# Cross attention with routing: where the routing pieces, the slot writes and GpSimd's elementwise work stand in a period

## The reference, cut to what matters

```python
q = split(x @ Wq + bq); k = split(ctx @ Wk + bk); v = split(ctx @ Wv + bv)
probs = softmax(q @ k.T / 4)            # layer 0: masked scores
x = layernorm(x + (probs @ v) @ Wo + bo)
scores = sigmoid(x @ gate_w.T)          # layer 1; layer 0: softmax of the best two
idx = top_k(scores + bias, K)           # the experts of a row
pos = cumsum(onehot(idx)) - 1           # the row's place within its expert
xe[idx, pos] = x                        # the rows written out by slot
```

## Time and profile before

| | us |
|---|---|
| median of 3 runs (lowest, highest) | 3422.43 (3417.75, 3429.29) |
| the profiled execution | 3419.93 |
| its span, first to last instruction | 3418.2 |
| PE, DVE, ACT, POOL busy | 2593.2, 2067.1, 1100.1, 817.1 |
| mean granted clock of TensorE, share of full speed | 0.872 |

### The profile page before, as it was taken

The page is one execution under the profiler, slowest core; times in us unless marked ns, Lnnn a source line. Parts: engine busy times, 40 slices in busy tenths (PEclk is TensorE's granted clock), DMA queues, the critical chain, the costliest instruction groups (busy, mean ns, idle before and its releaser), DMA issues. The chain is left out here.

```text
span 3418.2 us, 51809 instructions
## 1 busy us (share of the span) xinstructions
PE 2593.2 (76%) x17697; PEld 2118.0 (62%) x17698; DVE 2067.1 (60%) x4570; ACT 1100.1 (32%) x1952; POOL 817.1 (24%) x932
## 2 busy tenths in 40 slices
PE   4788786799999599988888989776758878747500
PEld 3666664455555499988888989755635555536400
DVE  5888885345555476666666665465536676635554
ACT  2334342344444222211111112123625454425400
POOL 0000000111111152222121020252112444332575
PEclk8999997899999699999999999888869888758855
DMA  1100020534432300012011010210055544327887
GB/s 50 34 18 21 18 71 28 76 56 63 66 54 32 111 31 31 28 61 90 25 61 61 31 61 28 57 54 20 0 82 88 91 75 64 48 49 201 215 119 90
DMA packets 201924, 210.31 MB, mean 62 GB/s; under 512 B 39889, under 2 KB 188152, under 8 KB 201808
## 3 DMA queue, kind: packets, MB, share of 16 engines
q1 hardware_dynamic: 166352, 142.53, 20.2%
q0 software_dynamic: 18432, 36.94, 6.2%
q10 hardware_dynamic: 17024, 29.36, 2.5%
HBM read 103.42 MB, written 67.90 MB: 50 GB/s over the span
## 5 line engine op out<-in xcount | busy, mean ns | idle before, releaser
L1143 DVE TENSOR_REDUCE x_nmx<-x_ps 128x4 f32<-128x1024 f32 x256 | 313.1, 1223 | 376.0 <-PE x_ps L879 374.8
L1497 PE MATMUL m_gu<-m_x_hi,m_w_hi 128*128 128x256 f32 x1632 | 464.8, 285 | 28.0 <-DVE m_x_lo L1563 17.5
L1497 PE MATMUL m_gu<-m_x_hi,m_w_lo 128*128 128x256 f32 x1632 | 459.9, 282 | 0.0
L1497 PE MATMUL m_gu<-m_x_lo,m_w_hi 128*128 128x256 f32 x1632 | 459.5, 282 | 0.0
L1535 ACT ACTIVATE m_sg<-m_gu 128x256 f32<-128x256 f32 x408 | 156.7, 384 | 754.7 <-PE m_gu L1497 754.7
L1047 ACT ACTIVATE x_pt<-x_ps 128x1024 f32<-128x1024 f32 x256 | 262.1, 1024 | 298.4 <-PE x_ps L879 295.9
L1569 DVE TENSOR_TENSOR m_h<-m_sg,m_gu 128x256 f32<-128x256 f32 x408 | 171.5, 420 | 306.6 <-ACT m_sg L1535 304.4
L1497 PEld LDWEIGHTS m_gu<-m_x_hi,m_w_hi 128*128 128x128 f32 x1632 | 312.0, 191 | 32.7 <-DVE m_x_lo L1563 17.9
L1497 PEld LDWEIGHTS m_gu<-m_x_hi,m_w_lo 128*128 128x128 f32 x1632 | 311.9, 191 | 0.0
L1497 PEld LDWEIGHTS m_gu<-m_x_lo,m_w_hi 128*128 128x128 f32 x1632 | 311.5, 191 | 0.0
L1486 PE MATMUL m_yp<-m_w_hi,m_h_hi 128*128 128x256 f32 x816 | 244.4, 299 | 80.2 <-DVE m_h_lo L1571 80.2
(11 more groups left out here) (301 smaller groups left out, 5477.1 us busy)
## 6 DMA issues: line engine op xcount, KB each, us to landing
m_x<-xs SPq DMA_DIRECT2D x68, 256.0 KB, 2.8
ys<-m_y SPq DMA_DIRECT2D x67, 256.0 KB, 2.2
x_qpack<-x_qh SPq DMA_DIRECT2D x128, 128.0 KB, 4.0
x_kpack<-x_kh SPq DMA_DIRECT2D x128, 128.0 KB, 4.3
xs<-zero SPq DMA_DIRECT2D x8, 1024.0 KB, 5.1
x_cx<-in_ctx SPq DMA_DIRECT2D x32, 256.0 KB, 5.3
x_qpack<-x_ql SPq DMA_DIRECT2D x64, 128.0 KB, 5.1
x_kpack<-x_kl SPq DMA_DIRECT2D x64, 128.0 KB, 5.3
```

What stands on the lines that cost most here:

```text
L1143: dve.tensor_reduce(nmx[:, n % U, t, 0:HEADS].rearrange("p (m q b) -> p m q b", m=2, q=QUADS)[:, :, j, :], ps[:, QUERY:QUERY + 2].rearrang ...
L1497: ins = pe.matmul(gu[:, m % 4, n, :], wp[n][:, c, m * P:m * P + P], xp_[:, c, :], start=(c == 0 and k == 0), stop=(c == KC - 1 and k == 2))
```

## The change

It moves pieces and adds waits; no arithmetic is added or removed. DVE: `place` goes one period later, between maximum 0 and maximum 1; `choose` is cut at the one-hot rows, of which the second part (`one_hot`) stands ahead of maximum 5; `weigh_experts` moves ahead of maximum 6; `take_logits` reads the logits in both layers. PE: `turn_rows`, `route`, `output`, `rank`, `weigh(k, 1)` and `key_scores(l, 7)` change places; ACT follows. POOL: the eight slot writes of a batch come a period later in two lots of four, one behind `low_queries`, one behind `rstd_of`; and each of the three large operations first waits until the scores of a certain group are ready, which is when that group's maximum begins (group 2, 4 and 5). One period is added for the drain.

```diff
--- before.py
+++ after.py
@@ -709,7 +709,7 @@
         ctx_v = d["ctx"].rearrange("(k p) n -> p k n", p=P)
         shared_v = st.xsh.rearrange("(n p) c -> p n c", p=P)
 
-        PERIODS = range(-1, B + 3)
+        PERIODS = range(-1, B + 4)
 
         def blocks(n):
             return slice(TB * n, TB * n + TB)
@@ -785,43 +785,52 @@
 
         @block.gpsimd
         def _(pool):
+            def beside_maximum(q, g):
+
+                if 0 <= q < B:
+                    pool.wait_ge(s_ready, GROUPS * q + g + 1)
+
             def low_queries(n):
                 pool.wait_ge(qh_ready, n + 1)
                 if n:
                     pool.wait_ge(pack_loaded[(n - 1) % PACKS], 16 * PACK_DMAS * ((n - 1) // PACKS + 1))
+                beside_maximum(n - 1, 2)
                 pool.tensor_tensor(ql[:], qf[:], qh[:].bitcast(F32), ALU.subtract).then_inc(ql_ready, 1)
 
             def low_keys(n):
                 pool.wait_ge(kh_ready, n + 1)
+                beside_maximum(n - 1, 4)
                 pool.tensor_tensor(kl[:], kf[:], kh[:].bitcast(F32), ALU.subtract).then_inc(kl_ready, 1)
 
             def add_bias(n):
                 if n >= U:
                     pool.wait_ge(xn_ready, n - U + 1)
+                beside_maximum(n + 2, 5)
                 pool.tensor_tensor(y[:, n % U], st.res[:, blocks(n), :], rows[:, 1:2, :].to_broadcast([P, TB, D]),
                                    ALU.add).then_inc(xb_ready, 1)
 
             def rstd_of(n):
                 pool_rstd(pool, st, var, rstd, n % U, varr, rstdr, epsr, n + 1)
 
-            def slots_out(n):
+            def slots_out(n, t):
                 pool.wait_ge(dst_ready, n + 1)
                 pool.sem_inc(st.pool_passed, 1)
-                for t in range(TB):
-                    for j in range(topk):
-                        pool.indirect_dma_start(
-                            out=st.xs1, out_offset=bass.IndirectOffsetOnAxis(ap=st.slot1[:, TB * n + t, j:j + 1], axis=0),
-                            in_=st.res[:, TB * n + t, :], in_offset=None, bounds_check=DUMP1 - 1,
-                            oob_is_err=False).then_inc(sent, 16)
+                for j in range(topk):
+                    pool.indirect_dma_start(
+                        out=st.xs1, out_offset=bass.IndirectOffsetOnAxis(ap=st.slot1[:, TB * n + t, j:j + 1], axis=0),
+                        in_=st.res[:, TB * n + t, :], in_offset=None, bounds_check=DUMP1 - 1,
+                        oob_is_err=False).then_inc(sent, 16)
 
             pool.wait_ge(w_loaded, 16 * 4)
             for p in PERIODS:
                 at(p + 1, low_queries)
+                if not masked:
+                    at(p - 4, slots_out, 0)
                 at(p + 1, low_keys)
                 at(p - 2, add_bias)
                 at(p - 2, rstd_of)
                 if not masked:
-                    at(p - 3, slots_out)
+                    at(p - 4, slots_out, 1)
             if not masked:
                 pool.wait_ge(sent, 16 * TB * topk * B)
 
@@ -967,16 +976,16 @@
                 at(l, weigh, 2)
                 at(a, turn_in)
                 at(k, turn_maxima)
+                at(l, key_scores, 7)
+                at(q, query_scores, 0)
+
+                at(a, project_queries)
                 at(r, turn_rows)
-                at(q, query_scores, 0)
-
-                at(l, key_scores, 7)
-                at(a, project_queries)
                 at(q, query_scores, 1)
 
                 at(l, weigh, 3)
+                at(k, key_scores, 0)
                 at(r, route)
-                at(k, key_scores, 0)
                 at(q, query_scores, 2)
 
                 at(k, key_scores, 1)
@@ -994,12 +1003,12 @@
                 at(q, query_scores, 5)
 
                 at(k, key_scores, 4)
+                at(l, output)
+                at(r, rank)
+                at(q, query_scores, 6)
+
+                at(k, key_scores, 5)
                 at(k, weigh, 1)
-                at(l, output)
-                at(q, query_scores, 6)
-
-                at(k, key_scores, 5)
-                at(r, rank)
                 at(q, query_scores, 7)
             if masked:
                 pe.wait_ge(counted, 1)
@@ -1075,31 +1084,31 @@
                 at(l, keep_values, 2)
                 at(a, keep_rows)
                 at(k, keep_maxima)
+                at(l, weights, 7)
+
+                at(a, keep_queries)
                 at(r, keep_normal)
-
-                at(l, weights, 7)
-                at(a, keep_queries)
 
                 at(l, keep_values, 3)
                 at(k, weights, 0)
+
+                at(k, weights, 1)
                 if not masked:
                     at(r, gates)
-
-                at(k, weights, 1)
                 at(a, keep_keys)
 
                 at(k, weights, 2)
                 at(k, keep_values, 0)
+
+                at(k, weights, 3)
                 if masked:
                     at(r, gates)
-
-                at(k, weights, 3)
                 at(l, keep_scaled)
 
                 at(k, weights, 4)
+
+                at(k, weights, 5)
                 at(k, keep_values, 1)
-
-                at(k, weights, 5)
 
         @block.vector
         def _(dve):
@@ -1168,13 +1177,16 @@
             def spread(v, shape):
                 return v.unsqueeze(3).to_broadcast(shape)
 
+            def take_logits(n):
+                dve.wait_ge(lg_ready, n + 1)
+                logits = bank(ROUTE)[:, :, 0:experts]
+                if masked:
+                    dve.tensor_copy(lg[:, :, 0:experts], logits).then_inc(lg_taken, 1)
+                else:
+                    dve.tensor_scalar(sc[:], logits, -1.0, EXP_MAX, ALU.mult, ALU.min).then_inc(lg_taken, 1)
+
             def choose(n):
-                u, here = n % U, blocks(n)
-                logits = bank(ROUTE)[:, :, 0:experts]
-                chosen = st.expert0[:, here, :] if masked else ixf[:]
                 if masked:
-                    dve.wait_ge(lg_ready, n + 1)
-                    dve.tensor_copy(lg[:, :, 0:experts], logits).then_inc(lg_taken, 1)
                     dve.wait_ge(lg_taken, n + 1)
                 else:
                     dve.wait_ge(e_ready, n + 1)
@@ -1190,6 +1202,10 @@
                     s.mark(dve.max_index(ix8[:, t, :], mx8[:, t, :], lg[:, t, :]))
                 if masked:
                     dve.tensor_tensor(tmp[:, :, 0], mx8[:, :, 1], mx8[:, :, 0], ALU.subtract).then_inc(earg_ready, 1)
+
+            def one_hot(n):
+                u, here = n % U, blocks(n)
+                chosen = st.expert0[:, here, :] if masked else ixf[:]
                 s.after(s.n)
                 s.do(dve.tensor_copy(chosen, ix8[:, :, 0:topk]))
                 s.do(dve.tensor_tensor(oh[:], st.iota[:, 0:ecols].unsqueeze(1).unsqueeze(1).to_broadcast([P, TB, topk, ecols]),
@@ -1215,12 +1231,6 @@
                     s.do(dve.tensor_scalar(tmp[:, :, 0], tmp[:, :, 0], 1e-12, None, ALU.max))
                     s.do(dve.reciprocal(tmp[:, :, 1], tmp[:, :, 0]))
                     s.do(dve.tensor_tensor(gt[:], gt[:], tmp[:, :, 1:2].to_broadcast([P, TB, topk]), ALU.mult))
-
-            def exponents(n):
-                dve.wait_ge(lg_ready, n + 1)
-                if n:
-                    dve.wait_ge(hit_ready, n)
-                dve.tensor_scalar(sc[:], bank(ROUTE)[:, :, 0:experts], -1.0, EXP_MAX, ALU.mult, ALU.min).then_inc(lg_taken, 1)
 
             def place(n):
                 here = blocks(n)
@@ -1249,20 +1259,20 @@
                 a, q, l, r = p + 1, p, p - 2, p - 3
                 at(r, normalize)
                 at(q, maxima, 0)
+                at(r - 1, place)
                 at(q, maxima, 1)
-                if not masked:
-                    at(r, exponents)
+                at(r, take_logits)
                 at(q, maxima, 2)
                 at(r, choose)
                 at(q, maxima, 3)
                 at(l, scaled)
                 at(q, maxima, 4)
-                at(r, weigh_experts)
+                at(r, one_hot)
                 at(q, maxima, 5)
                 at(a, values)
+                at(r, weigh_experts)
                 at(q, maxima, 6)
                 at(l, add_output)
-                at(r, place)
                 at(q, maxima, 7)
             if masked:
 
```

More of the change, by code:

```diff
@@ L996, in _ @@
                 at(k, key_scores, 4)
-                at(k, weigh, 1)
                 at(l, output)
+                at(r, rank)
                 at(q, query_scores, 6)
                 at(k, key_scores, 5)
-                at(r, rank)
+                at(k, weigh, 1)
                 at(q, query_scores, 7)
@@ L1077, in _ @@
                 at(k, keep_maxima)
-                at(r, keep_normal)
                 at(l, weights, 7)
                 at(a, keep_queries)
+                at(r, keep_normal)
                 at(l, keep_values, 3)
                 at(k, weights, 0)
+                at(k, weights, 1)
                 if not masked:
                     at(r, gates)
```

(1 more changed line is left out.)

## The result

The changed kernel takes 3323.67 us (median of 4 runs, 3317.87 to 3327.77), the kernel before 3420.88 beside it (3417.75 to 3429.29): ratio 0.9711, 95% interval 0.9686 to 0.9735. That is 97 us less, where 74 were forecast, and 2.3 us under the low end of the range. The profiled execution took 3320.87 us, its span is 3319.2.

What follows compares the result with a forecast made beforehand. Layer 0 was taken as PE-bound, layer 1 as DVE and PE waiting in turn. Gains of 66 (periods of 23.3 + 1.0 + 0.7 = 25.0 us), 3 and 5 made 74 us: 3348 us, range 3326 to 3376.

Steps and rivals of the forecast that it cites:

- the twelve periods: Layer 1's window of twelve periods: from 30.5 to 25.0 us each, a gain of 66 us.
- the part behind them: Layer 1 from maximum 0 of batch 15 on: 3 us gained in a partial period, drain 0 within 3.
- signs that I had set down for being wrong: Idle over 1.5 us before maximum 2 or 3, many `one_hot` stalls, low clock in most periods, drain over 6 us longer.
- The chain of 23.3 us: One new layer 1 period with nothing in its way, summed piece by piece: 23.3 us, DVE busy for 21.
- The meeting of kl with `one_hot`: Layer 1: POOL's late kl runs over DVE's `one_hot`; 1.0 us a period, bounds nothing and 1.28.
- The part I had excluded: Layer 1: POOL's y starts with maximum 5 and ends as `values` begins, so no cost in `one_hot`.
- The low clock: Layer 1, PE at scores 6 and 7: a low stretch every other period, 0.7 us, bounds 0 and about 2.5.
- my bound of 0.86 us: PE standstill ahead of scores 6 and 7: 0.86 us passed at the full clock, 2.80 us did not.
- The step that failed: Layer 0, bound by PE: an order can win only 0.46 us per period, 5 us over 12 periods.
- The drains: Layer 1's end: 5 us more slot writes against about as much from `place`, 0 within 3; layer 0's had no term.
- Rival 1: Layer 1: slot writes grow by about 1.3 us a lot and kl covers all of `one_hot`; 3359 us, chance 0.12.
- Rival 2: Layer 1: POOL and DVE never meet, clock full; 23.3 to 24.2 us a period, 3328 to 3334 us, chance 0.18.

Runs made afterwards that it cites:

- e8: Changed kernel with POOL's list laid out so that no large operation meets a DVE piece with two SBUF operands: 3287.12 us.
- e7: Kernel before with DVE's new order, all eight slot writes in one lot a period later, no holds; PE, ACT and POOL otherwise in the old order: 3339.2 us.
- e5: Kernel before with the new order of PE and ACT alone; DVE and POOL as before: ratio 0.9979 to the kernel before.
- c1: Kernel before, unchanged, run again on a second chip: median 3408.62 us, layer 1 at 575.0 us.
- c2: Changed kernel, unmodified, run again on a second chip: ratio 0.9737 to the kernel before, layer 1 at 500.8 us.
- e9: Changed kernel without the holds and with all eight slot writes in one lot behind the reciprocal root: 3361.34 us.
- e6: Changed kernel, holds kept, with all eight slot writes in one lot behind the reciprocal root: 3319.3 us.
- e1: Changed kernel without POOL's waits for a group's scores, lots kept: ratio 0.9639 to the kernel before, on a slower chip.
- e4: Kernel before with `place` and all eight slot writes a period later, nothing else moved: ratio 0.9915 to the kernel before, on a slower chip.

## Why the prediction was right and where it failed

**The sign and the mechanism** held: `place` left the front of the last maximum, PE no longer stands still there, and layer 1 became DVE-bound. Layer 1 as a whole came out nearly as forecast, 67.7 us less against 69, but by two errors that cancel: the twelve periods gained 54.5 us of 66, the part behind them 11.5 in place of 3. Two of the signs that I had set down for being wrong came: stalled instructions in `one_hot`, in eleven of twelve periods, and the low clock in most of them.

**The chain of 23.3 us** was right. e8, in which nothing meets, has 23.24. Single steps, in e8, as distance from the maximum before (forecast, measured): maximum 1 3.35, 3.38; maximum 2 2.05, 2.30; maximum 3 3.7, 3.47; maximum 4 2.2, 2.20; maximum 5 2.75, 2.72; maximum 6 3.55, 3.50; maximum 7 2.95, 2.93; maximum 0 2.75, 2.74.

**The meeting of kl with `one_hot`** was forecast, at 1.0 us a period; it costs 1.48 (4.20 less 2.72). The part I had excluded, y in `one_hot`, is half of it: I took y to "start with maximum 5", but the semaphore counts PE's scores. **The low clock**: forecast 0.7 us a period; the period of batches 5 to 14 averages 26.36 us, which leaves 26.36 - 23.23 - 1.48 = 1.65 us. (The one period with the meeting and the full clock throughout, that of batch 4, takes 24.71, which is 23.23 + 1.48.) The place was right (a standstill of PE ahead of scores 7 between 0.86 and 2.80 us), the frequency not, because the meeting itself makes that standstill longer: 1.77 us with it, 0.85 without, and e8 with 0.85 keeps the full clock in this window. The length alone doesn't decide, as my bound of 0.86 us had it: e7 lost the clock behind 0.77 to 0.88 us four times in twelve, and the changed kernel kept it behind 1.77 three times in eleven. So two terms that I added up separately are in large part one. The kernel before had it already: in its four periods with a meeting PE stands still for 2.86 us, and maximum 5 comes 4.41 us behind maximum 4, not 2.84.

**The step that failed** is in layer 0: "0.46 us per period is all that an order can win there", read off a PE busy for 339.24 of 344.30 us. It won 1.03 us a period, 30.26 us where I had set down 30.8 to 31.3: 14.9 us from batch 0 to 15 against 5. With the drains, below, that took layer 0 to 23.0 us in place of 5. The time is 2.3 us under the range, so this step alone would explain it; but the 8 us of the last stage, which are not the change's, would too. Without them the time would have been 3332, inside the range for all the errors in it. The ends of matmuls are modelled, and a modelled end covers a stall behind it. The starts show it. PE in layer 0 of the kernel before:

```profile
818.73 0.17 PE L961 MATMUL x_ps<-x_hit,lower 128*128 128x8 bf16 x1
819.04 0.60 PE L875 MATMUL x_ps<-x_mb,identb 128*128 128x512 bf16 x2
...
822.47 0.38 PE L895 MATMUL x_ps<-ident,x_nmx 128*128 128x128 f32 x2
823.02 0.66 PE L838 MATMUL x_ps<-ident,res 128*128 128x128 f32 x4 [0.16 <-DVE res L202]
823.64 0.59 PE L875 MATMUL x_ps<-x_mb,identb 128*128 128x512 bf16 x2
```

and the changed kernel, where the mask product follows both pieces and the rows are transposed elsewhere:

```profile
811.38 0.17 PE L970 MATMUL x_ps<-x_hit,lower 128*128 128x8 bf16 x1
811.40 0.59 PE L884 MATMUL x_ps<-x_mb,identb 128*128 128x512 bf16 x2
...
817.76 0.38 PE L904 MATMUL x_ps<-ident,x_nmx 128*128 128x128 f32 x2
817.98 0.60 PE L884 MATMUL x_ps<-x_mb,identb 128*128 128x512 bf16 x2
```

From start to start 0.31 became 0.02 behind `rank`, and 0.55 became 0.22 behind `turn_maxima`; in the kernel before the transposition of rows took 0.62, and the same helper has a pitch of 0.43 where nothing is waited for (811.50 to 811.93, transposing `aq`); and a group of scores had 0.65 (800.47 to 801.12) in place of 0.43. The sum is 0.29 + 0.33 + 0.19 + 0.22 = 1.03 us, the whole gain of a period; 0.46 of it were idle time in the records, the rest lay under modelled ends. e5 shows that it is the order of PE and ACT, e7 that DVE's order adds none.

**The drains.** That of layer 1 was put at 0 within 3, behind 3 us for batch 15; that of layer 0 stood in the sum at nothing, with no reason given. From maximum 0 of batch 15 on they gave 11.5 and 8.5 us. In layer 0 it is PE's order again: e5 has most of it (72.1 us, against 78.6 in c1 and 70.0 in c2). In the periods without maxima PE used to wait for `normalize` in front of `turn_rows` and then for ACT; the rows are of the kernel before, then of the changed one:

```profile
1101.13 0.66 PE L838 MATMUL x_ps<-ident,res 128*128 128x128 f32 x4 [0.79 <-DVE res L202]
...
1103.78 1.07 PE L912 MATMUL x_ps<-x_pt,x_vp 128*32 128x256 f32 x16 [1.12 <-ACT x_pt L1047]
```

```profile
1086.00 0.66 PE L847 MATMUL x_ps<-ident,res 128*128 128x128 f32 x4
1087.19 1.07 PE L921 MATMUL x_ps<-x_pt,x_vp 128*32 128x256 f32 x16 [0.53 <-ACT x_pt L1056]
```

In layer 1, from maximum 0 of batch 15: c1 99.5, e7 97.4, e5 94.3, e9 91.7, e6 91.1, c2 86.7 us. So the orders of PE, ACT and DVE give 8 and the two lots about 5; I had counted the lots as a cost. I had priced what the new place of `place` adds to the drain and not what PE's order takes from it.

**The slot writes** beside `place` and `choose` take 0.97 to 1.05 us but for the one beside `normalize` (1.16): 1004 ns on average against 984. Rival 1, and the rule of the Trainium skill (SBUF — State Buffer, "SBUF: two separate sides") that it was set beside, did not come about: the writes were not late. What met was the other direction of the same section: it says that the pair of ports that GpSimd and VectorE share is an exclusive lock for whole instructions, against VectorE operations with two SBUF inputs too. The stalls of additions and products in this case agree with it (0.18 to 0.86, 0.41 to 1.26, each until a POOL operation ends). The length of the stall in e9 is more than one instruction's: there three POOL operations passed.

**Rival 2** (no meeting, the clock full) did not happen in the changed kernel, though the time came out near its 3328; e8 is that case, and the gains of layer 0 and of the drains put it lower still.

**Parts.** Layer 1's gain is DVE's order (e7). The new order of PE and ACT is worth 21 us in layer 0 (e5 against c1) and costs layer 1 10 us by itself (e5 against c1, where kl and y meet `choose` more often) and 41 beside DVE's new order (e9 against e7), since `choose` then starts later and meets ql. The holds bring 38 of the 41 back (e6 against e9) and the lots 4 more, in the drain. The two are not independent: in e1, lots without holds, nothing meets, and it is as short although signals are late there. So beside the lots the holds may cost more than they bring; that was not tested on a chip without the late signals. What `place` alone gives can't be read from e4, where the late signals lie in the way.

## What to carry to other kernels

Where an engine looks full, take the ceiling of a new order from start-to-start distances of the same piece with and without a wait, not from its busy share. Treat a stall and the lower clock behind it as one term: the stall lengthens the time that PE stands, and with it the chance of the lower clock, though a short standstill is no guarantee (e7). A wait placed to keep two engines apart must count the event of the engine to be avoided (here DVE's own `hit_ready`), not that of its supplier, which runs ahead as soon as the other is the bound.

## What the runs showed of the hardware

- A DVE addition of 0.23 us did not get its turn between three POOL operations of 128x512 that followed each other without a gap: 4.47 us on average, nine times of nine (e9). By the records it had begun 0.65 us before the first of them, beside a slot write, and at 0.23 us would have ended before it; starts on POOL are rough in a profile, and why it lost is open.
- Maxima and `values`, which read PSUM, kept 1.22 and 0.74 us beside a POOL operation; a cast of 8 columns in SBUF went from 0.17 to 0.95 us.
- PE standstills of 0.85 us left the clock at 2.4 GHz through eleven periods (e8), but in e7 four of twelve of 0.77 to 0.88 us were followed by a stretch at 1.2 GHz; so were eight of eleven of 1.77 us (changed kernel) and eight of ten of about 2 us (e6).
- On the occasion of e1 to e4 and on no other, ACT and DVE went on waiting for work of PE after its record had ended, beside rows of slot writes: in the period shown of e4 for 5.4 us (2868.62 to 2873.98), in that of e1 for about 1.5; unexplained.
